# A decoder block on one core: the gelu's quantisation scaling computed on VectorE instead of GpSimd

## The reference

```python
def mx_quant(x):                       # blocks of BLOCK = 32 along the last axis, BITS = 8
    amax = jnp.max(jnp.abs(xb), axis=-1, keepdims=True)
    shared_exp = jnp.floor(jnp.log2(jnp.where(amax > 0, amax, 1.0)))
    scale = jnp.exp2(shared_exp - (BITS - 2))
    q = jnp.clip(jnp.round(xb / scale), -2.0 ** (BITS - 1), 2.0 ** (BITS - 1) - 1) * scale
...
    h = mx_layernorm(x, ln_w, ln_b)
    h = mx_linear(h, W1, b1)           # 512 -> 2048
    h = mx_gelu(h)
    h = mx_linear(h, W2, b2)           # 2048 -> 512, its input goes through mx_quant
    return bf16_round(residual + h)
```

## Time and profile before

| | |
|---|---|
| median of 3 runs | 1302.64 us (1300.14 to 1305.56) |
| profiled execution, its own time | 1298.63 us |
| span in the profile | 1296.8 us |
| TensorE busy | 1228.5 us (95%) |
| VectorE busy | 1105.2 us (85%) |
| ScalarE busy | 815.1 us (63%) |
| GpSimd busy | 643.5 us (50%) |
| mean granted TensorE clock | 0.987 |

### The profile page before, as it was taken

One profiled execution on the slowest core, in us unless ns is written; L12 is line 12 of the kernel. 1 busy time (PEld: TensorE's weight loads), 2 busy tenths in 40 slices (PEclk: granted clock), 3 DMA queues, 4 the chain that ended last, 5 costly groups with the idle time before them and its releaser, 6 DMA issues.

```text
span 1296.8 us, 34522 instructions
## 1 busy us (share of the span) xinstructions
PE 1228.5 (95%) x13320; PEld 794.0 (61%) x13352; DVE 1105.2 (85%) x1912; ACT 815.1 (63%) x1581; POOL 643.5 (50%) x703
## 2 busy tenths in 40 slices
PE   5888999999999999999999999999999999999874
PEld 4657666666676556667666666766666676566421
DVE  7887989889888889888888888889888888898775
ACT  5456757576666676667666666666676665675541
POOL 8866354646455444555444445454435544455323
PEclk9999999999999999999999999999999999999987
DMA  8755142212223221222222122232222122212222
GB/s 274 222 144 119 37 82 68 62 45 63 53 82 73 69 69 27 70 73 70 53 78 61 47 57 70 78 65 65 59 55 65 53 63 76 73 43 46 70 64 53
DMA packets 137330, 97.08 MB, mean 75 GB/s; under 512 B 108112, under 2 KB 110160, under 8 KB 136400
## 3 DMA queue, kind: packets, MB, share of 16 engines
q1 hardware_dynamic: 137168, 94.87, 28.5%
HBM read 37.16 MB, written 8.39 MB: 35 GB/s over the span
## 4 chain that ended last, share of the span: by engine, by line
PE 83%; DVE 6%; issue 3%; DMA 3%; POOL 2%; ACT 1%; SPq 1%; POOLq 0%; DVEq 0%; ACTq 0%
PE bank_b L746 16%; PE bank_y L800 8%; PE bank_a L746 8%; PE bank_a L736 8%; PE bank_y L864 7%; PE rt L828 5%; PE rt L815 5%; PE rt L765 5%; PE bank_o L834 5%; PE bank_b L855 4%; PE bank_a L855 4%; PE bank_o L792 2%; PE bank_y L784 2%; DMA gmem<-w 2%; DVE negm L1998 1%
## 5 line engine op out<-in xcount | busy, mean ns | idle before, releaser
L4969 POOL TENSOR_TENSOR gmem<-gmem,unit_g 128x1024 bf16<-128x1024 bf16 x64 | 124.5, 1947 | 210.9 <-DVE unit_g L2051 210.9
L1998 DVE TENSOR_REDUCE negm<-rt 128x16 f32<-128x2048 f32 x64 | 146.3, 2286 | 10.4 <-PE rt L815 10.1
L3692 ACT ACTIVATE pT<-rt 128x2048 f32<-128x2048 f32 x64 | 120.1, 1876 | 42.7 <-PE rt L828 28.6
L746 PE MATMUL bank_a<-mix_r,w_Wr 128*128 128x128 f32 x1024 | 121.8, 277 | 2.8 <-POOL mix_r L4928 2.8
L746 PEld LDWEIGHTS bank_b<-mix_k,w_Wk 128*128 128x128 f32 x1024 | 120.2, 195 | 5.7 <-issue 5.6
L746 PE MATMUL bank_b<-mix_k,w_Wk 128*128 128x128 f32 x1024 | 121.4, 278 | 2.0 <-DVE mix_k L1946 2.0
L746 PEld LDWEIGHTS bank_a<-mix_r,w_Wr 128*128 128x128 f32 x1024 | 117.0, 192 | 9.8 <-issue 8.0
L864 PE MATMUL bank_y<-w2q,gmem 128*128 128x512 bf16 x480 | 112.8, 383 | 7.9 <-DMA gmem<-gmem 5.1
L746 PE MATMUL bank_b<-mix_g,w_Wg 128*128 128x128 f32 x1024 | 120.0, 275 | 0.0
L736 PE MATMUL bank_a<-w_Wv,mix_v 128*128 128x512 f32 x256 | 117.3, 601 | 2.2 <-ACT rT L3618 2.2
L800 PE MATMUL bank_y<-w_Wo,yT 128*128 128x512 f32 x256 | 116.1, 596 | 3.2 <-DVE yT L1985 3.2
(11 more groups left out here) (263 smaller groups left out, 2842.4 us busy)
## 6 DMA issues: line engine op xcount, KB each, us to landing
qx<-qdense SPq DMA_DIRECT2D x64, 224.0 KB, 3.3
context<-ctx SPq DMA_DIRECT2D x32, 384.0 KB, 3.3
xin<-x SPq DMA_DIRECT2D x32, 256.0 KB, 3.3
gmem<-w SPq DMA_DIRECT2D x16, 512.0 KB, 4.5
out<-x SPq DMA_DIRECT2D x32, 256.0 KB, 2.3
vp<-vz SPq DMA_DIRECT2D x32, 128.0 KB, 2.9
odense<-oT SPq DMA_DIRECT2D x128, 32.0 KB, 2.0
pT<-Wv SPq DMA_DIRECT2D x1, 1024.0 KB, 8.6
```

The costliest lines, as they stand in the source:

```text
L746: done = e.matmul(bank[:, m * T:(m + 1) * T], wt[f"W{name}"][:, c, m * P:(m + 1) * P], mix[name][:, c, :], start=(c == 0), stop=(c == KT - 1))
L1998: e.tensor_reduce(negm[:, 0:H].rearrange("p (g a j) -> p g j a", g=4, a=2)[:, :, 2 * i:2 * i + 2, :], rt[:, :].rearrange("p (g j a s) -> p ...
L3692: e.activation(pT[:, :, :].rearrange("p g n -> p (g n)"), rt[:, :], ACT.Exp, scale=float(D) ** -0.5).then_inc(sem(f"act_ex{i}"), 1)
L4969: e.tensor_tensor(blocks(half), blocks(half), per_block(unit[f"g{i}"], 32), ALU.mult).then_inc(sem(f"pool_gsc{i}"), 1)
```

## The change

The call `gelu_scale` leaves GpSimd's list. Its multiply is made in `gelu_round` on VectorE instead, right in front of the clip: read in pairs (`in_pairs`, `pair_per_block`) and written as 16-bit integers over the half. The clip then works on integers. The calls of all engines keep their order; `dve_gchain` counts five steps a sequence, and `pool_gsc` is gone.

```diff
             def gelu_round(n, i):
                 half = g_bf[:, 2 * C * i:2 * C * (i + 1)]
-                e.wait_ge(sem(f"pool_gsc{i}"), n + 1)
-                e.tensor_scalar(half.bitcast(I16), half, MOST, None, ALU.min).then_inc(sem(f"dve_gchain{i}"), 1)
+                whole = half.bitcast(I16)
+                e.wait_ge(sem(f"dve_gchain{i}"), 5 * n + 3)
+                e.tensor_tensor(in_pairs(whole), in_pairs(half), pair_per_block(unit[f"g{i}"], 32),
+                                ALU.mult).then_inc(sem(f"dve_gchain{i}"), 1)
+                e.wait_ge(sem(f"dve_gchain{i}"), 5 * n + 4)
+                e.tensor_scalar(whole, whole, MOST, None, ALU.min).then_inc(sem(f"dve_gchain{i}"), 1)
...
-            def gelu_scale(n, i):
-                half = g_bf[:, 2 * C * i:2 * C * (i + 1)]
-                e.wait_ge(sem(f"dve_gchain{i}"), 4 * n + 3)
-                e.tensor_tensor(blocks(half), blocks(half), per_block(unit[f"g{i}"], 32),
-                                ALU.mult).then_inc(sem(f"pool_gsc{i}"), 1)
...
             second_sum(1)
-            gelu_scale(0, 0)
             gate_parts(3)
```

More of the change, by code:

```diff
@@ L2086, in gelu_pow2 @@
             def gelu_pow2(n, i):
-                block_floor(f"g{i}", f"dve_gchain{i}", 4 * n + 1)
-                block_pow2(f"g{i}", 32, f"dve_gchain{i}", 4 * n + 2).then_inc(sem(f"dve_gchain{i}"), 1)
+                block_floor(f"g{i}", f"dve_gchain{i}", 5 * n + 1)
+                block_pow2(f"g{i}", 32, f"dve_gchain{i}", 5 * n + 2).then_inc(sem(f"dve_gchain{i}"), 1)
             def gelu_round(n, i):
                 half = g_bf[:, 2 * C * i:2 * C * (i + 1)]
-                e.wait_ge(sem(f"pool_gsc{i}"), n + 1)
-                e.tensor_scalar(half.bitcast(I16), half, MOST, None, ALU.min).then_inc(sem(f"dve_gchain{i}"), 1)
+                whole = half.bitcast(I16)
[4 more added lines that the diff above has]
+                e.tensor_scalar(whole, whole, MOST, None, ALU.min).then_inc(sem(f"dve_gchain{i}"), 1)
             def gelu_quantised(n, i):
                 half = g_bf[:, 2 * C * i:2 * C * (i + 1)]
-                e.wait_ge(sem(f"dve_gchain{i}"), 4 * n + 4)
+                e.wait_ge(sem(f"dve_gchain{i}"), 5 * n + 5)
                 e.tensor_tensor(in_pairs(half), in_pairs(half.bitcast(I16)), pair_per_block(pow2[f"g{i}"], 32),
@@ L5196, in _ @@
             gate_rstd(17)
-            gelu_scale(14, 1)
-            gelu_scale(15, 0)
             with_bias(19)
@@ L5206, in _ @@
             gate_rstd(18)
-            gelu_scale(15, 1)
-            gelu_scale(16, 0)
             with_bias(20)
@@ L5216, in _ @@
             gate_rstd(19)
-            gelu_scale(16, 1)
-            gelu_scale(17, 0)
             with_bias(21)
@@ L5226, in _ @@
             gate_rstd(20)
-            gelu_scale(17, 1)
-            gelu_scale(18, 0)
             with_bias(22)
@@ L5236, in _ @@
             by_parity(22)
-            gelu_scale(18, 1)
-            gelu_scale(19, 0)
             with_bias(23)
@@ L5246, in _ @@
             gate_rstd(22)
-            gelu_scale(19, 1)
-            gelu_scale(20, 0)
             with_bias(24)
@@ L5256, in _ @@
             by_parity(24)
-            gelu_scale(20, 1)
-            gelu_scale(21, 0)
             with_bias(25)
@@ L5266, in _ @@
             by_parity(25)
-            gelu_scale(21, 1)
             mixed(26, "r")
-            gelu_scale(22, 0)
             last_sum(21)
@@ L5276, in _ @@
             gate_rstd(25)
-            gelu_scale(22, 1)
             mixed(27, "r")
-            gelu_scale(23, 0)
             second_sum(24)
@@ L5285, in _ @@
             mixed(27, "g")
-            gelu_scale(23, 1)
-            gelu_scale(24, 0)
             mixed(28, "r")
@@ L5293, in _ @@
             by_parity(28)
-            gelu_scale(24, 1)
             with_bias(27)
@@ L5298, in _ @@
             with_bias(28)
-            gelu_scale(25, 0)
             second_sum(26)
@@ L5305, in _ @@
             gate_rstd(28)
-            gelu_scale(25, 1)
             last_sum(24)
             with_bias(30)
-            gelu_scale(26, 0)
             mixed(30, "r")
@@ L5316, in _ @@
             by_parity(30)
-            gelu_scale(26, 1)
             with_bias(31)
-            gelu_scale(27, 0)
             mixed(31, "r")
@@ L5323, in _ @@
             by_parity(31)
-            gelu_scale(27, 1)
             gate_rstd(30)
```

36 lines of the change are left out of this document (removed).

## The result

The changed kernel takes 1308.20 us, median of 20 runs (1303.38 to 1316.33); the kernel before took 1302.22 us beside it, also 20 runs. The ratio is 1.0050, 95% interval 1.0038 to 1.0062: slower by 5 to 8 us, about 6.5. The forecast was +3.0 us. The median lies in its range and at the edge of the 0.5% that the prediction counted as no change; the size is off by a factor of two. In this text an execution is one launch of a kernel, and only one launch of each has a trace.

What follows compares the result with a forecast made beforehand. TensorE was taken to bound the middle, chains through all engines the tail. Small margins +2.5, a removed collision -0.7 and the tail +1.2 summed to +3.0 us on the 1302.64 us median: 1305.6 us, range 1299 to 1313.

Steps and rivals of the forecast that it cites:

- kind 2: Middle, small margins before TensorE: two places read off, 0.9 us, four more estimated, 1.6; together +2.5, bounds 0.9 and 9.
- What bounds the kernel: From 120 to 1200 us TensorE bounds, missing only 6.06 us; the last 96.8 us are bound by chains through all engines.
- The multiply's price: Each of 64 added VectorE multiplies takes 0.69 us alone, 0.75 with collisions; 48 us in all.
- Kind 1: Middle: places where the added 0.75 us fits into VectorE's idle time, 5 us a sequence against 1.5 us added.
- The place at 600 us: Clip at 599.67 right ahead of the score maximum L1998, margin 0.17 us: TensorE waits 0.58 us.
- The place at 319 us: Clip at 306.41 delays the quantised hidden's transpose, needed by TensorE at 319.18; margin 0.46, so 0.3 us.
- Kind 3: At 1112.10 us L1985 no longer collides with GpSimd's scaling: -0.7 us, bounds 0 and -1.4, as L4974 may come back.
- The tail: Added multiplies in the last sequences' chains delay the last 16 matmuls: +1.2 us, bounds 0.5 and 2.5.
- (a): VectorE becomes the bound in many sequences: 12.4 us, 1315.0; or a half-rate product, about 1318; chance 0.22 (0.18 and 0.04).
- (b): Released collisions with GpSimd make it faster, all together -8 us, 1294.6; decides from 6.5 us on; chance 0.06.
- (c): All hidden, 0 us, 1302.6; chance 0.72 together with the forecast, between 1296.1 and 1309.1.
- The signs: What would show it: VectorE near 1150 us, GpSimd near 519, TensorE busy 1228.5, two-input groups' means within 100 ns.

Runs made afterwards that it cites:

- the real pair: The traced executions of the kernel before and the changed kernel, both with transposing DMAs; medians 1302.22 and 1308.20 us.
- the base: The kernel before with plain DMAs in place of all transposing ones, output not the reference's: 1300.86 us, ratio 0.9991 to the kernel before.
- the run with the six alone: Against the plain-DMA kernel before, scaling on VectorE only at (2,1), (3,1), (7,0), (12,0), (18,0), (25,0), sequence and half: 1304.93 us.
- (25,1) run: Against the plain-DMA kernel before, scaling on VectorE only for the second half of sequence 25: 1299.76 us.
- the tail run: Against the plain-DMA kernel before, scaling on VectorE only for sequences 28 to 31: 1302.80 us.
- the 50 others: Against the plain-DMA kernel before, scaling on VectorE for sequences 0 to 27 except six places ahead of steps: 1299.23 us.
- reordering around them: Against the plain-DMA kernel before, the full change with ten calls moved in VectorE's list, four `gelu_round` calls in the middle among them: 1304.34 us.

## Why the prediction was right, and where its sizes were off

The forecast was +3.0 us and about +6.5 was measured. Each of its three terms had the right sign. The range held the result because it was wide: its upper side came from the bound of 9 us for kind 2, not from the sum. That bound of the sum, 11.5, added to 1302.6 even gives 1314.1, more than the 1313 that is said to hold it.

- **What bounds the kernel.** Right. TensorE's work is unchanged, and all that the change did in the middle was to add and to remove waits.
- **The multiply's price.** Right: 742 ns for the 0.75 taken, 0.68 alone. The integer output costs no half rate.
- **Kind 1, hidden.** Right: 50 of 56 multiplies cost nothing together.
- **Kind 2, the small margins.** This is the term that was mis-sized. The forecast had six places and +2.5 us, two read from rows and four estimated; there are six, and they measure +4.05 in the real pair (0.36, 0.66, 0.51, 0.66, 1.06, 0.8), 4.8 on the base. That the number of places agrees is in part luck: one of the two that were read off didn't come. The place at 600 us was forecast at 0.58 and measured 0.66. The place at 319 us didn't come: TensorE's matmul there is 1.38 us late, as much as it had been since 291 us. What the estimate of 0.3 to 0.6 each left out is that the added instruction can collide with what GpSimd still does (1.33 us for 0.69), and can push the next VectorE instruction into a collision too (2.48 us for 1.58): the second makes the 1.06 at 837 us, where the clip had been slow before. Nor is the 0.36 at 250 us the multiply's own delay: TensorE waits there for the hidden's transfer, and ahead of it L2063 took 1.40 us at 243.18, 0.41 before, beside GpSimd's mixing, and the last product 1.48 us at 244.78, 0.68 before; what brought the two together was argued, not tested. The number of places is shown by the run with the six alone, the collisions by the rows.
- **Kind 3, the collision removed.** The mechanism was right, the size was -0.7 for a measured -1.35 (0.82 and 0.53). L4974, which I feared would come back, did both things: it came back ahead of L1985 (the powers of the hidden, 1.08 us for 0.18), where 0.58 of the 1.40 us stayed, and it left L2068 behind L1985 (1.64 us to 0.68), where it had stood before, which gave 0.53 more; the prediction hadn't seen the second. The rule of the Trainium skill ("SBUF — State Buffer", section "SBUF: two separate sides"), that the two engines shut each other out for a whole instruction, gave -1.4 for L1985 alone. The rows agree with it at L1985 (2.40 us beside the scaling, 0.68 without), but that -1.35 comes near -1.4 is luck: it is the sum of two places. The (25,1) run shows the first on the base, -0.81, with the same 0.58 left. The rule also covers the collisions of kind 2, which I did not go on to price with it.
- **The tail.** +1.2 forecast; +3.02 in the profiled pair, +1.9 by the medians of the tail run. The last chain was followed well: the two multiplies give 0.72 and 0.71, the 1.5 forecast for the last 16 matmuls, which in all start 2.7 us later against the projection of 1194.60 us. Left out were the waits ahead of it, 1.0 us, of which 0.24 can be traced to a multiply, 0.51 is a slower transfer and 0.25 stays open. The longer spell at the lower clock, which the prediction had only as its upper bound, gives some 0.6 us. So about 1.1 us of the pair's tail, the transfer and the clock, isn't work that the change added; whether the change brings on the longer spell isn't shown.
- **The rivals.** (a) is out at this load, by the steps and by the 50 others; the clip done twice shows that it is near. (b), the release of collisions, is real, by the step of 0.8 at 1116 us, but small: 2.8 us by the medians with the scaling left out, not the 8 that it could have been. (c) is out by the interval.
- **The signs.** TensorE's busy time was to stay at 1228.5 us and is 1232.0: it rose with the time at the lower clock. L2093, named there among the two-input groups, has one input; its mean went from 551 to 539 ns.

Sum of the real pair: middle 3.43 (4.4 in the eight steps up, 0.4 in smaller ones, less 1.35), tail 3.02; together 6.45. That this meets the measured 6.5 so closely is chance, since it is one pair of executions and holds 1.3 us (the step at 145 us, the transfer, the clock) that isn't the multiply's delay; the medians alone differ by 6.0.

## What to carry to other kernels

Moving work to an engine that is 85% busy and whose order is fixed costs nothing at most places and its full price, or twice that, at a few. The sum of busy times says nothing about which. Subtract the starts of the bound engine's stretches in the two traces: the steps name the places. Here, giving back the six and the tail did better (1299.2 us) than reordering around them (1304.3), though it doesn't clearly beat the kernel without the change. A step counts only if it repeats: transfers and the clock make steps of 0.3 to 1.6 us of their own. An instruction that is moved into the shadow of a wait can meet the other engine's work there, and its neighbour with it.

## What the runs showed of the hardware

- VectorE's one-input 16-bit instructions are slower beside GpSimd too: a clip that takes 0.42 us alone takes 539 to 564 ns on average, and 487 with the scaling left out on both engines; powers of 128x32 took 1.08 us beside a sum of GpSimd and 0.18 without.
- A plain DMA between two SBUF tiles of 256 KB lands in 2.3 us (median) where the transposing one takes 3.1; at half the size it is 2.0 for 2.4.
- Two executions of one kernel (the base) differ by 1.4 us in the middle and 1 us in the tail, with the same instructions in the same order. In six tails of the same code the length, 104.3 to 107.3 us, follows the time that TensorE works at a granted clock of 0.50, 10.1 to 20.4 us.
